# A fused conv-attention and routed-FFN kernel: another order of all engines' steps, nine images per loop pass, the extra matmuls shifted to the expert steps

## Time and profile before

| | |
|---|---|
| median of three runs | 11223.81 us |
| profiled execution | 11266.36 us |
| its span | 11264.6 us |
| PE busy | 10212.1 us (91%) |
| VectorE, ScalarE, GpSimd busy | 57%, 50%, 47% |
| mean granted TensorE clock | 0.764 |

### The profile page before, as it was taken

The page is one execution under the profiler, slowest core; times in us unless marked ns, Lnnn a source line. Parts: engine busy times, 40 slices in busy tenths (PEclk is TensorE's granted clock), DMA queues, the critical chain, the costliest instruction groups (busy, mean ns, idle before and its releaser), DMA issues. The chain is left out here.

```text
span 11264.6 us, 258378 instructions
## 1 busy us (share of the span) xinstructions
PE 10212.1 (91%) x65865; PEld 7901.0 (70%) x65865; DVE 6405.5 (57%) x26878; ACT 5624.9 (50%) x12484; POOL 5302.4 (47%) x7260
## 2 busy tenths in 40 slices
PE   6899999999999999999999999999999999998655
PEld 5677777777777777777777777777777777776444
DVE  5766665565555566566666556665656666555200
ACT  3655555455554555555555555554555555544211
POOL 2455554454444455455445545544545555444321
PEclk9978777787777787777788778876778887776555
DMA  0000000000000000000000000000000000000000
GB/s 21 8 10 16 17 17 15 15 19 16 16 17 17 15 18 17 16 17 17 16 17 19 17 15 17 17 17 15 17 17 18 18 16 17 16 15 16 21 18 10
DMA packets 222474, 183.89 MB, mean 16 GB/s; under 512 B 63337, under 2 KB 193331, under 8 KB 220552
## 3 DMA queue, kind: packets, MB, share of 16 engines
q1 hardware_dynamic: 161128, 84.94, 3.1%
q0 software_dynamic: 59680, 79.82, 2.5%
...
## 5 line engine op out<-in xcount | busy, mean ns | idle before, releaser
...
L611 PE MATMUL ps<-we_hi,identh 128*128 128x512 f16 x4096 | 1558.7, 470 | 94.3 <-issue 93.8
L1423 POOL DMA_INDIRECT slots<-rec,slot x1024 | 1053.2, 1029 | 971.7 <-issue 871.1
L1601 ACT ACTIVATE ht<-ps,be 128x128 f32<-128x128 f32 x3252 | 1061.0, 368 | 688.0 <-issue 408.9
L830 PE MATMUL ps<-we,ht 128*128 x6504 | 1313.7, 368 | 0.0
L830 PEld LDWEIGHTS ps<-we,ht 128*128 128x128 f32 x6504 | 1177.3, 271 | 146.4 <-issue 104.3
L1450 POOL DMA_INDIRECT out_y<-ys,row_at x813 | 870.6, 1071 | 787.3 <-DMA out_y<-ys,row_at 430.1
L816 PE MATMUL ps<-xs,we_hi 128*128 128x128 f16 x3252 | 758.6, 250 | 481.1 <-issue 342.8
L665 PEld LDWEIGHTS ps<-vexp,pt 98*98 98x98 f32 x8192 | 991.6, 194 | 139.8 <-issue 106.8
L1300 DVE TENSOR_TENSOR yv<-ps,rt 128x384 f32<-128x384 f32 x271 | 151.1, 558 | 1608.4 <-PE ps L830 1608.4
L646 PE MATMUL ps<-kexp,qbd 128*98 128x392 f32 x2048 | 1027.3, 587 | 40.9 <-issue 16.2
L665 PE MATMUL ps<-vexp,pt 98*98 98x36 f32 x8192 | 971.2, 270 | 0.0
(10 more groups left out here) (232 smaller groups left out, 22854.4 us busy)
## 6 DMA issues: line engine op xcount, KB each, us to landing
...
xg<-in_x SPq DMA_DIRECT2D x256, 98.0 KB
...
lw<-tile_list SPq DMA_DIRECT2D x271, 0.0 KB
...
tile_list<-entry SPq DMA_DIRECT2D x64, 0.5 KB
```

The costliest lines, as they stand in the source:

```text
L611: pe.matmul(bank[:, :], identh[:, :], we1[0][:, 0:512], start=True, stop=True)
L830: last = pe.matmul(dst, ht[:, q, 2 * e + h, :], we2[:, bass.ds(chosen[q][e] * 2 + h, 1), :].rearrange("p a c -> p (a c)"), start=False, st ...
L1423: pool.indirect_dma_start(slots, bass.IndirectOffsetOnAxis(ap=slot[:, j % 2, t:t + 1], axis=0), rec[:, bass.ts(j % RB, 1), t, :].rearrange ...
L1601: act.activation(ht[:, q, b, :], pH[:, 128 * b:128 * (b + 1)], ACT.Gelu, bias=be1[:, bass.ds(chosen[q][b // 2] * 2 + b % 2, 1)], scale=1.0 ...
```

## The change

Every list of `ORDER` gets another order, and some steps work on another group (`tk` from -9 to -11, `lo` and `hi` from -11 to -10, `t`, `stu`, `st2`, `rt12` and `zT` by one; `hnt1` moves to the start of ScalarE's next iteration). The eight fillers have other places and banks, and all stand at -26: by `runs_at` a step at -26 runs where expert step n - 26 exists, so in iterations 26 to 296, where before they ran in 0 to 255. `HANDED` gets the entries that the new order needs. The steady loop runs up to nine images per pass; 27 steady images make three passes.

```diff
         ORDER = dict(
-            pe="""mix0:+0 fO0:+0 tx:-26 lp:-10 fO1:+0 ei0:-26 pT0:+1 fA0:+0 q:+2 k:+2 fS0:+0 mix1:+0 rk:-11 ei1:-26 fY0:+0
-                  pT1:+1 s0:+2 o0:+1 z2T:+0 pT2:+1 fS1:+0 fc10:+0 o1:+1 fc11:+0 s1:+2 mix2:+0 xnT:-10 pT3:+1 ei2:-26 s2:+2
-                  uT:-1 mix3:+0 o2:+1 logit:-10 s3:+2 v:+2 kv:-1 hT0:+0 o3:+1 hT1:+0 mix4:+0 eo0:-26 fc2:+0 eo1:-26 oT:+1
-                  fO2:+0 eo2:-26 proj:+1 G:-1 fS2:+0 zT:+3""",
+            pe="""mix0:+0 fY0:-26 zT:+2 lp:-10 tx:-26 pT0:+1 q:+2 k:+2 fH0:-26 fS0:-26 rk:-11 ei0:-26 mix1:+0 fS1:-26
+                  pT1:+1 fS2:-26 z2T:+0 o0:+1 s0:+2 pT2:+1 o1:+1 fc10:+0 fc11:+0 mix2:+0 ei1:-26 fB0:-26 pT3:+1 xnT:-10
+                  s1:+2 o2:+1 mix3:+0 uT:-1 o3:+1 logit:-10 s2:+2 kv:-1 ei2:-26 mix4:+0 eo0:-26 hT0:+0 hT1:+0 eo1:-26
+                  s3:+2 v:+2 eo2:-26 fA0:-26 oT:+1 fK0:-26 G:-1 proj:+1 fc2:+0""",
...
-            pool="""r3:-1 pw3:-1 ri:-27 tu:-3 sub1:+1 sub2:+1 sub3:+1 sc0:-12 dm00:-12 dm10:-13 dm20:-14 dm30:-15 dm40:-16
-                    dm50:-17 dm60:-18 r1:+3 r2:+0 pw2:+0 sc1:-12 dm01:-12 dm11:-13 dm21:-14 dm31:-15 dm41:-16 dm51:-17
-                    dm61:-18 pw1:+3 ru:-1 rx:-10 pwu:-1 so0:-27 pwx:-10 x1b:+0 sc2:-12 dm02:-12 dm12:-13 dm22:-14 dm32:-15
...
+            pool="""sub1:+1 r3:-1 sub2:+1 tk:-11 pw3:-1 sub3:+1 ri:-27 sc0:-12 dm00:-12 dm10:-13 dm20:-14 dm30:-15
+                    dm40:-16 dm50:-17 dm60:-18 tu:-3 r2:+0 pw2:+0 sc1:-12 dm01:-12 dm11:-13 dm21:-14 dm31:-15 dm41:-16
+                    dm51:-17 dm61:-18 so0:-27 rx:-10 ru:-1 pwx:-10 pwu:-1 r1:+3 sub0:+2 pw1:+3 so1:-27 sc2:-12 dm02:-12
...
         LAST_FLUSH = TOTAL + NP // 4 - 1
         SCATTER_TO_LOAD = 13
         STEADY = 4
+        IMAGES_PER_PASS = 9
...
             for i in range(-1, STEADY):
                 image(i)
-            with eng.Fori(STEADY, IMAGES - 1) as i:
-                image(i, STEADY)
+
+            steady = IMAGES - 1 - STEADY
+            body = max(d for d in range(1, IMAGES_PER_PASS + 1) if steady % d == 0)
+            with eng.Fori(0, steady // body) as i:
+                for part in range(body):
+                    image(i * body + (STEADY + part), STEADY)
             for i in range(IMAGES - 1, (STEPS + 26) // GROUPS + 1):
                 image(i)
```

More of the change, by code:

```diff
@@ L371, in build @@
-            act="""hi:-11 ve:+1 ot:+0 exp:+1 zt:+2 xc:-26 lpg:-10 h00:-26 h01:-26 pt0:+1 h02:-26 h03:-26 ke:+2 pt1:+1
-                   utc:-9 h10:-26 h11:-26 z2t:+0 h12:-26 ge0:+0 pt2:+1 om0:+1 h13:-26 xnt:-10 pt3:+1 ge1:+0 utk:-1 h20:-26
-                   h21:-26 sq:-1 tanh:-11 om1:+1 h22:-26 hnt0:+0 hnt1:+0 h23:-26 sd:-1""",
-            pool="""r3:-1 pw3:-1 ri:-27 tu:-3 sub1:+1 sub2:+1 sub3:+1 sc0:-12 dm00:-12 dm10:-13 dm20:-14 dm30:-15 dm40:-16
-                    dm50:-17 dm60:-18 r1:+3 r2:+0 pw2:+0 sc1:-12 dm01:-12 dm11:-13 dm21:-14 dm31:-15 dm41:-16 dm51:-17
-                    dm61:-18 pw1:+3 ru:-1 rx:-10 pwu:-1 so0:-27 pwx:-10 x1b:+0 sc2:-12 dm02:-12 dm12:-13 dm22:-14 dm32:-15
-                    dm42:-16 dm52:-17 dm62:-18 tk:-9 v0:-10 so1:-27 v1:-10 sub0:+2 so2:-27 sc3:-12 dm03:-12 dm13:-13
-                    dm23:-14 dm33:-15 dm43:-16 dm53:-17 dm63:-18""",
+            pe="""mix0:+0 fY0:-26 zT:+2 lp:-10 tx:-26 pT0:+1 q:+2 k:+2 fH0:-26 fS0:-26 rk:-11 ei0:-26 mix1:+0 fS1:-26
+                  pT1:+1 fS2:-26 z2T:+0 o0:+1 s0:+2 pT2:+1 o1:+1 fc10:+0 fc11:+0 mix2:+0 ei1:-26 fB0:-26 pT3:+1 xnT:-10
+                  s1:+2 o2:+1 mix3:+0 uT:-1 o3:+1 logit:-10 s2:+2 kv:-1 ei2:-26 mix4:+0 eo0:-26 hT0:+0 hT1:+0 eo1:-26
+                  s3:+2 v:+2 eo2:-26 fA0:-26 oT:+1 fK0:-26 G:-1 proj:+1 fc2:+0""",
@@ new lines, in build @@
+            dve="""st2:+0 mv2:+0 pk:-11 c2:+0 t2:-10 t:-1 mix0:+0 z2:+0 qbd:+2 sp:-11 stu:-1 mix1:+0 stx:-10 mvu:-1
+                   mvx:-10 cx:-10 cu:-1 ct:-11 sb0:+2 pa:-11 li:-11 mx0:+2 xn:-10 st30:+0 oj0:+1 u:-1 rc0:+1 mix2:+0
+                   mix3:+0 sa:-11 sb1:+2 c1:+3 st31:+0 mv3:+0 rt0:-10 on0:+1 rt1:-10 sl:-11 rt2:-10 oj1:+1 rt3:-10 rt4:-10
+                   rt5:-10 sb2:+2 rt6:-10 kvss:-1 mx1:+2 st1:+4 rt7:-10 rt8:-10 mx2:+2 z:+3 rt9:-10 rc1:+1 sb3:+2 kve:-1
+                   kvr:-1 on1:+1 kvn:-1 mx3:+2 rt10:-10 tw:-11 w:-11 lo:-10 Gsum:-1 rt11:-10 yv:-26 ya:-26 x1:+1 rt12:-10
+                   tr:+0 ys:-26 cd:-10 mv1:+4""",
@@ new lines, in build @@
+            act="""hnt1:-1 ve:+1 ot:+0 exp:+1 zt:+2 lpg:-10 pt0:+1 xc:-26 ke:+2 h00:-26 tanh:-11 pt1:+1 utc:-9 h01:-26
+                   h02:-26 z2t:+0 h03:-26 pt2:+1 ge0:+0 om0:+1 h10:-26 h11:-26 h12:-26 ge1:+0 pt3:+1 hi:-10 xnt:-10 utk:-1
+                   h13:-26 om1:+1 sq:-1 h20:-26 h21:-26 h22:-26 sd:-1 hnt0:+0 h23:-26""",
+            pool="""sub1:+1 r3:-1 sub2:+1 tk:-11 pw3:-1 sub3:+1 ri:-27 sc0:-12 dm00:-12 dm10:-13 dm20:-14 dm30:-15
+                    dm40:-16 dm50:-17 dm60:-18 tu:-3 r2:+0 pw2:+0 sc1:-12 dm01:-12 dm11:-13 dm21:-14 dm31:-15 dm41:-16
+                    dm51:-17 dm61:-18 so0:-27 rx:-10 ru:-1 pwx:-10 pwu:-1 r1:+3 sub0:+2 pw1:+3 so1:-27 sc2:-12 dm02:-12
+                    dm12:-13 dm22:-14 dm32:-15 dm42:-16 dm52:-17 dm62:-18 v0:-10 v1:-10 so2:-27 sc3:-12 dm03:-12 dm13:-13
+                    dm23:-14 dm33:-15 dm43:-16 dm53:-17 dm63:-18 x1b:+0""",
@@ L382, in build @@
         HANDED = dict(
-            fA0="zT_ready.0:+2 x1_ready.0:+0 oT_ready.0:+0 hnT_ready.1:-1 uT_kept.0:-2 hid_ready.1:-1 z2T_ready.0:-1 q_ready.0:+1",
+            fA0="hnT_ready.1:+0 uT_kept.0:-1 hid_ready.1:+0 z2T_ready.0:+0 q_ready.0:+2 zT_ready.0:+2 x1_ready.0:+0 oT_ready.0:+0",
+            zT="x1_ready.0:+0 oT_ready.0:+0 hnT_ready.1:-1 uT_kept.0:-2 hid_ready.1:-1 z2T_ready.0:-1 q_ready.0:+1 zT_ready.0:+1",
             q="zT_ready.0:+2 x1_ready.0:+0 oT_ready.0:+0 hnT_ready.1:-1 uT_kept.0:-2 hid_ready.1:-1 z2T_ready.0:-1 q_ready.0:+1",
@@ L390, in build @@
             proj="oT_ready.0:+1 hnT_ready.1:+0 uT_kept.0:-1 hid_ready.1:+0 z2T_ready.0:+0 q_ready.0:+2 zT_ready.0:+2 x1_ready.0:+0",
-            zT="x1_ready.0:+1 oT_ready.0:+1 hnT_ready.1:+0 uT_kept.0:-1 hid_ready.1:+0 z2T_ready.0:+0 q_ready.0:+2 zT_ready.0:+2",
+            fB0="hid_ready.0:+0 spot_ready.0+count_ready.0:-11 gelu_ready.0:-10 fc2_scaled.0:-1 hnT_ready.0:-1 logit_ready.0:-11 xnT_ready.0:-11",
             lp="fc2_scaled.0:-1 hnT_ready.0:-1 logit_ready.0:-11 xnT_ready.0:-11 hid_ready.0:-1 spot_ready.0+count_ready.0:-12 gelu_ready.0:-11",
@@ L398, in build @@
             fc2="hnT_ready.0:+0 logit_ready.0:-10 xnT_ready.0:-10 hid_ready.0:+0 spot_ready.0+count_ready.0:-11 gelu_ready.0:-10 fc2_scaled.0:-1",
+            fK0="kv_ready.0:-1 mix3:+0 mix2:+0 mix1:+0 mix0:+0 g_ready.0:-2",
             mix0="g_ready.0:-2 kv_ready.0:-2 mix3:-1 mix2:-1 mix1:-1 mix0:-1",
@@ L404, in build @@
             G="kv_ready.0:-1 mix3:+0 mix2:+0 mix1:+0 mix0:+0 g_ready.0:-2",
-            fO0="o_joined.1:+0 o_joined.0:+0 kexp_ready.0:+1",
-            fO1="o_joined.1:+0 o_joined.0:+0 kexp_ready.0:+1",
-            fO2="o_joined.1:+1 o_joined.0:+1 kexp_ready.0:+2",
             k="o_joined.1:+0 o_joined.0:+0 kexp_ready.0:+1",
@@ L416, in build @@
             fS0="score_bias.3:+1 score_bias.2:+1 score_bias.1:+1 score_bias.0:+1",
-            fS1="score_bias.0:+2 score_bias.3:+1 score_bias.2:+1 score_bias.1:+1",
-            fS2="score_bias.3:+2 score_bias.2:+2 score_bias.1:+2 score_bias.0:+2",
+            fS1="score_bias.3:+1 score_bias.2:+1 score_bias.1:+1 score_bias.0:+1",
+            fS2="score_bias.3:+1 score_bias.2:+1 score_bias.1:+1 score_bias.0:+1",
             s0="score_bias.3:+1 score_bias.2:+1 score_bias.1:+1 score_bias.0:+1",
@@ L422, in build @@
             s3="score_bias.2:+2 score_bias.1:+2 score_bias.0:+2 score_bias.3:+1",
-            fY0="xs_ready.0:-26 yv_ready.0:-27",
+            fY0="yv_ready.0:-27 xs_ready.0:-27",
             tx="yv_ready.0:-27 xs_ready.0:-27",
             eo0="xs_ready.0:-26 yv_ready.0:-27",
+            fH0="h_ready.11:-27 h_ready.7:-27 h_ready.3:-27",
             ei0="h_ready.11:-27 h_ready.7:-27 h_ready.3:-27",
```

## The result

The changed kernel takes 9950.92 us, median of four runs (9911.45 to 10012.18), the kernel before in the same set 11241.1: a ratio of 0.886, 95% interval 0.880 to 0.893. Some executions of a kernel are slower than the rest, by over 1.5% of its fastest; ratios leave them out, medians do not.

A forecast was written before the change was run, and what follows sets the result against it. PE's clock was taken to bound the kernel; -495 (middle, edges included) + 100 (start) + 50 (end) = -345, and 11266 - 345 - 43 gave about 10880 us, range 10380 to 11500.

The forecast's parts named there:

- What bounds the kernel: Middle of the kernel: PE, rarely idle, sets the pace through its clock, 44% of the time at the lower level.
- The share at the low clock: Middle: two of eight iterations lose their clock to idle time removed or shortened; share 0.44 to 0.41, -495 us, edges included.
- s: Share of time at the low clock in the middle's iterations: 0.44 before, taken as 0.41 after, bounds 0.30 and 0.52.
- F: Length of a middle iteration at full clock: from 32.9 to 31.7 us, bounds 30.9 and 32.9.
- the rival: Middle: the clock mostly holds, low share falls to 0.2, -1370 there, 10000 us in all; chance 0.13.
- Idle before expert and router steps: Full-clock iteration: PE's 2.03 us idle ahead of ei0, ei1, ei2 and xnT shrinks to 0.8.
- The slower rival: Middle: kv, ei2 and eo0 in a row drop the clock in most iterations, 11613 us; chance 0.24.
- The transposes: hT0 right ahead of hT1, between eo0 and eo1, could be a new place for the clock to fall; given no term.
- The loop's edges: Ends of loop passes: 24 fewer edges at 3.6 us idle each, 87 us less; longer straight code counted 0.
- The first 26 iterations: Start, left without fillers: +100 us, between -50 if the clock holds and +150 if it stays at 0.50.
- The last 41: Final iterations, now with fillers: +50 us, between +60 at the low clock and -115 if it rises for eo.
- What would show it: Signs: middle's clock 0.79 to 0.80; idle at fillers' line 7 us, line 816 under half, xnT under 80; start's clock near 0.6.

The follow-up runs named there:

- m2: The changed kernel with its last filler fK0 moved from behind oT to between logit and s2, still eight fillers: 9514.42 us, ratio 0.845.
- b1: The kernel before with pwx put ahead of pwu and so0 in GpSimd's list, nothing else: 10422.65 us, ratio 0.927.
- h_pool: The changed kernel with GpSimd's whole list from the kernel before, all other lists as changed: 10664.62 us, ratio 0.942.
- m4: The changed kernel with the place of ei2's tile read three times instead of once ahead of ei2, in PE's queue: 10980.84 us, ratio 0.969.
- b2: The kernel before with pwx ahead of pwu and so0 in GpSimd's list and nine images per pass: 10272.93 us, ratio 0.917.

## Why the prediction was wrong

**What bounds the kernel: right.** PE idles 254 us of 7899, and the clock and the length of a full-clock iteration give the time: 30.7 / (1 - 0.42 x 0.26) = 34.5 per iteration; measured 7899 / 229 = 34.5. (0.42 us lost per us at the low level is the fit over its iterations; the forecast had 0.45.)

**The share at the low clock: the step that failed.** The forecast kept s at 0.41 from 0.44; it is 0.26. It said that edges and mix iterations explain two of eight iterations, and that the run without a filler "still holds most of the iteration". The second part has a truth: 41 of 91 falls come there, at s2, and m2, which halves them and cuts what follows each from 29 to 3.4 us, takes 440 us off. The first part was the error. The ordinary iterations' low clock hung on xnT and ei2 as well: idle of 0.4 and 0.6 us, right ahead of thin steps. b1 shows it, with 784 us of middle for one move, and h_pool the same from the other side, 630 us of the whole. The forecast gave this move only its own idle time, in F. Its argument against the rival, that "at 0.44 the clock is low far longer than edges and mix steps explain", spoke for it once every iteration's short stalls are counted with their neighbours.

**Idle before expert and router steps: F was 31.7 in the forecast, 30.7 measured.** Of 32.9 - 30.7 = 2.2 us, the forecast had 1.2. xnT's 0.43 and ei1's 0.40 went as said. ei2 was to keep 0.5 and has none: kv, 1.04 us, hides the read. ei0 was to have 0.1 and has 0.54: the forecast read from two rows that this wait shrinks with the matmul time queued just before, and behind two fillers and rk it is as long as it was behind one filler. rk, right ahead of ei0, is seven short records; what sets this wait was not tested. A wait ahead of eo2 came, 0.35 in the mean. The term not thought of is the step itself: ei1 and ei2 each run 0.5 us faster with their registers read ahead, 1.0 in all.

**The slower rival** had the mechanism right and the place wrong: a stall at ei2 among kv, eo0, hT0 and eo1 does cost the clock, about 1000 us when m4 makes one, but the order removed it. Its cover is thin: two register reads more take back about three quarters of the gain.

**The transposes.** The changed kernel has no fall at hT0 or hT1, though eo0, hT0, hT1, eo1 stand in a row. By the Trainium skill ("TensorE: Matmul & The Clock Gate", Part 4) transposes do not count as busy in the way that other matmuls do, and in m4, with a stall ahead, 106 falls do stand at hT0 and hT1, but 80 at eo0, ahead of both. No run changes the transposes alone, so their part stays open.

**The loop's edges: right in their idle time**, 94 to 7 us for 87 forecast. With the clock they measured about 200 us in the old order and 40 to 110 in the new one, with overlapping intervals. Nine images' straight code shows no cost: b2 is no slower than b1.

**The first 26 iterations: +100 forecast, +146 measured**, at the worst bound. The sign was right and the reason mostly not: giving the fillers back returns 25 to 43.

**The last 41: +50 forecast, +20 measured**, of which the fillers are +37 (980 against 943); the clock does rise, 0.64 against 0.50 before.

**What would show it:** the middle's 0.87 lies between the forecast's 0.80 and the rival's 0.9. The fillers' line has 7 us of idle and xnT's 14, as listed; ei's line has 124 of 207, not under half, because ei0 kept its wait. The start's clock, 0.56, is as listed, the end's 0.64 is not 0.5. No third of the idle came back ahead of proj, fc2 or eo2; ahead of eo2 63 of 254 us did, a quarter.
